# Linear attention and butterfly feed-forward on one core: a new slot table for the feed-forward work of the last four chunks

## What is computed

```python
qkv = x @ W_qkv                                  # 16 heads of 64
q, k = relu(q @ W_f + b_f), relu(k @ W_f + b_f)
kv  = einsum('bhnd,bhne->bhde', k, v)
out = einsum('bhnd,bhde->bhne', q, kv) / (einsum('bhnd,bhd->bhn', q, k.sum(2)) + 1e-6)
x   = layernorm(x + out.reshape(...) @ W_out + b_out)
h   = gelu(butterfly(x @ W_exp + b_exp, up_weights) + up_bias)      # 512 hidden
x   = layernorm(x + butterfly(h, down_weights) @ W_con + b_con + down_bias)
```

## The kernel before

| chunk | x1T_lo | up tiles | down | transpose_y, residual |
|---|---|---|---|---|
| 4 | 33 | 33, 34, 35, 36 | 37 | 38 |
| 5 | 37 | 37, 38, 39, 40 | 41 | 42 |
| 6 | 41 | 41, 41, 42, 42 | 43 | 44 |
| 7 | 45 | 45, 45, 45, 45 | 46 | 47 |

## Time and profile before

### The profile page before, as it was taken

One profiled execution on the slowest core, in us unless ns is written; L12 is line 12 of the kernel. 1 busy time (PEld: TensorE's weight loads), 2 busy tenths in 40 slices (PEclk: granted clock), 3 DMA queues, 4 the chain that ended last, 5 costly groups with the idle time before them and its releaser, 6 DMA issues.

```text
span 379.0 us, 5158 instructions
## 1 busy us (share of the span) xinstructions
PE 333.4 (88%) x1841; PEld 235.3 (62%) x1841; DVE 246.2 (65%) x489; ACT 173.0 (46%) x289; POOL 80.6 (21%) x77
## 2 busy tenths in 40 slices
PE   4898999299799999999999999999979788589481
PEld 3765677176567767777767675776856565356250
DVE  3536999999956384666518774685585783882613
ACT  2531344034455564674645464646546543434120
POOL 3080565896300002001001100110110110111201
PEclk9999999879989999999999999999999989659766
DMA  5940509333902800630450046006505607500000
GB/s 176 302 143 32 191 17 315 113 112 117 214 9 48 179 0 2 149 78 2 112 115 0 2 110 144 2 3 139 113 2 123 132 3 164 116 0 0 29 28 28
DMA packets 25089, 33.73 MB, mean 89 GB/s; under 512 B 3656, under 2 KB 13928, under 8 KB 25064
## 3 DMA queue, kind: packets, MB, share of 16 engines
q1 hardware_dynamic: 24904, 33.38, 34.6%
q10 hardware_dynamic: 160, 0.03, 0.0%
HBM read 31.04 MB, written 2.36 MB: 88 GB/s over the span
## 4 chain that ended last, share of the span: by engine, by line
PE 52%; DVE 28%; issue 7%; DMA 6%; POOL 4%; ACT 2%; SPq 1%; POOLq 0%; DVEq 0%
PE ring L483 18%; PE kx_ps L555 9%; PE attn_ps L483 8%; DVE late L914 6%; PE ring L643 5%; DMA recips<-recip_rows 4%; DVE qn L995 3%; POOL rstd L462 3%; DVE stats L1004 3%; PE ring L535 2%; PE ring L575 2%; DVE bias_row_term L930 2%; PE desk L492 2%; DVE k_total L969 2%; DVE y_dn L918 2%
## 5 line engine op out<-in xcount | busy, mean ns | idle before, releaser
L765 ACT ACTIVATE q<-ring,bf_col 128x512 f32<-128x512 f32 x64 | 43.9, 686 | 52.3 <-PE ring L483 51.9
L555 PE MATMUL kx_ps<-k,xs 128*128 128x512 f32 x128 | 60.2, 593 | 0.8 <-ACT k L758 0.8
L751 ACT ACTIVATE qn_h<-qn 128x512 fp32r<-128x512 f32 x64 | 39.8, 627 | 36.7 <-DVE qn L995 36.7
L758 ACT ACTIVATE k<-ring 128x512 f32<-128x512 f32 x64 | 38.3, 598 | 34.2 <-PE ring L535 33.8
L901 DVE TENSOR_TENSOR qn_l<-qn,qn_h 128x512 fp32r<-128x512 f32 x64 | 42.9, 680 | 15.8 <-ACT qn_h L751 15.0
L459 POOL TENSOR_TENSOR var_eps<-mean_var,ln_eps 128x4 f32<-128x4 f32 x16 | 7.1, 443 | 205.0 <-DVE mean_var L1008 205.0
L995 DVE TENSOR_TENSOR qn<-q,recips 128x512 f32<-128x512 f32 x64 | 41.1, 684 | 10.5 <-DMA recips<-recip_rows 10.5
L451 POOL TENSOR_TENSOR y<-hid,y_up 128x512 f32<-128x512 f32 x18 | 38.3, 2150 | 39.8 <-DMA hid<-in_L_ffn_up_weights_dram 39.7
L555 PEld LDWEIGHTS kx_ps<-k,xs 128*128 128x128 f32 x128 | 24.1, 189 | 19.2 <-issue 16.5
L483 PE MATMUL ring<-xT_h,wq_h 128*128 128x512 f32 x64 | 35.9, 561 | 0.0
L483 PE MATMUL attn_ps<-qn_h,m_h 128*128 128x512 f32 x64 | 29.2, 456 | 7.6 <-DVE qn_l L901 3.9
(11 more groups left out here) (125 smaller groups left out, 549.7 us busy)
## 6 DMA issues: line engine op xcount, KB each, us to landing
recips<-recip_rows SPq DMA_DIRECT2D x32, 512.0 KB, 7.3
hid<-in_L_ffn_up_weights_dram SPq DMA_DIRECT2D x9, 512.0 KB, 5.3
x<-_L_ffn_down_weights_dram SPq DMA_DIRECT2D x9, 512.0 KB, 4.1
xs<-in_L_attn_x_dram SPq DMA_DIRECT2D x4, 512.0 KB, 7.4
out_dram<-y SPq DMA_DIRECT2D x8, 256.0 KB, 6.1
q<-in_L_attn_W_qkv_dram SPq DMA_DIRECT2D x2, 512.0 KB, 7.9
q<-in_L_attn_W_qkv_dram SPq DMA_DIRECT2D x2, 256.0 KB, 3.3
q<-in_L_attn_W_out_dram SPq DMA_DIRECT2D x2, 256.0 KB, 8.8
```

The lines of the kernel that those rows point to most:

```text
L555: t_.matmul(kx_ps[half], xs[b % XBUF][:, t, :], k[kt % KRING][:, half * CH:(half + 1) * CH], start=t == 0, stop=t == TILES - 1).then_inc(s ...
L751: a_.activation(dst, src, ACT.Copy).then_inc(done, 1)
L758: a_.activation(k[kt % KRING][:, half * CH:(half + 1) * CH], bank(("k", kt, half))[:, :], ACT.Relu).then_inc(s_taken, 1)
L765: a_.activation(q[:, i % QRING, :], bank(("q", i))[:, :], ACT.Relu, bias=bf_col[:, :])\
```

## The change

The tables of chunks 0 to 3 stay as they were. Those of chunks 4 to 7 are given by hand:

```diff
-    for n in range(ALLCH):
-        per = [1, 1, 1, 1, 1, 1, 2, 4][n]
+    for n in range(ALLCH - 4):
         at = ATTN_LAST[n] + 3
         for i in range(HT):
-            UPS.setdefault(at + i // per, []).append(HT * n + i)
-        DOWN_SLOT[at + HT // per] = n
-        YT_SLOT[at + HT // per + 1] = n
+            UPS[at + i] = [HT * n + i]
+        DOWN_SLOT[at + HT] = n
+        YT_SLOT[at + HT + 1] = n
+
+    for n, ups, down, back in [(4, [33, 34, 35, 35], 36, 37), (5, [37, 37, 38, 38], 39, 43),
+                               (6, [41, 41, 42, 42], 43, 45), (7, [45, 45, 45, 45], 46, 47)]:
+        for i in range(HT):
+            UPS.setdefault(ups[i], []).append(HT * n + i)
+        DOWN_SLOT[down] = n
+        YT_SLOT[back] = n
```

## The result

367.87 us, median of 4 runs (366.48 to 369.69), against 381.08 (380.1 to 384.87, a fourth run of the kernel before added): ratio 0.9638, 95% interval 0.9559 to 0.9717. The two medians alone give 0.965. The forecast was 368.3 with a range of 364.8 to 374.8. The profiled execution took 367.46, its span is 365.6 (forecast 366.35, before 379.0). Lines after the tables have moved down by 6: L483 is L489 now, L643 is L649, L995 is L1001.

A forecast was written before the change was run, and what follows sets the result against it. VectorE and TensorE wait for each other by turns. The last up tiles start 10.35 us earlier and take 2.3 less: span 379.0 - 10.35 - 2.3 = 366.35, with 1.9 around it 368.3 us, range 364.8 to 374.8.

The forecast's parts named there:

- Slots 35 and 36: Extra up tile and down projection of chunk 4 come early: norm(7) ends at 310.5, x1T_lo at 317.35.
- Slot 37: Second norm of chunk 4, nearly free in the DMA wait; first qn at 322.9 instead of 321.38, 1.5 lost.
- Slot 38: Without a norm it takes 2.6 us on VectorE; the next slot begins at 325.5 instead of 328.17.
- Slot 39: VectorE's norm takes 6.8 us plus 0.2 waiting; down(5), from 327.2 to 330.7, is hidden and 4.69 us leaves the chain.
- Slots 40 to 42: Up tiles begin at 337.0; six products take 4.2 us plus 1.7 for half clock, to 342.9; before, 349.2.
- Slots 43 to 45: add_x(7) from 343.5, residual(5) behind it, x1T_lo to 350.6; last up tiles start at 351.1, 10.35 us earlier.
- The last up tiles: In slot 45, at full clock: 2.8 + 0.2 instead of 5.27 us, 2.3 less (bounds 0 and 2.5).
- down(5) isn't hidden: Rival: from slot 39 half clock until chunk 5's down projection is over, up tiles 5 later; 373.3 us, chance 0.13.
- Only the order at the end counts: Rival: TensorE's work bounds slots 38 to 42, only slots 43 to 45 are shortened; 376.9 us, chance 0.13.
- Half clock all through: Rival: the clock never comes back from slot 39 on; 386.4 us, 1.4% slower, chance 0.05.

The follow-up runs named there:

- e10: Changed kernel with 15 more matmuls, read by nobody, behind down(5) in slot 39; ratio to before 0.9715.
- e11: Changed kernel with chunk 5's up tiles in 37 to 40 and its down in 41, as before; ratio to before 0.9707.
- e1: Kernel before with chunk 4's part of the change alone (fourth up tile in 35, down in 36, back in 37); ratio to before 0.9897.
- e2: Kernel before with chunk 5's up tiles in 37 and 38 and its down in 39 alone; ratio to before 0.9918.
- e9: Changed kernel with chunk 4 as it was before (fourth up tile 36, down 37, back 38); ratio to before 0.9712.
- e13: Kernel before with 13, 4 and 2 more matmuls, read by nobody, at the ends of slots 38, 39 and 40; ratio to before 0.997.
- e6: Kernel before with 22 more matmuls, read by nobody, in TensorE's idle time of slot 44; ratio to before 0.9925.
- e12: Changed kernel with the ways back of chunks 5 and 6 in slots 42 and 44 as before; ratio to before 0.9855.
- e4: Changed kernel with chunk 6's way back in slot 44 again; ratio to before 0.9781.

## Why the prediction was right

The time, 367.87 against 368.3, and the mechanism hold. By its own steps, with what each measured:

- *Slots 35 and 36.* norm(7) from 308.92 to 310.9 (forecast end 310.5), x1T_lo of chunk 5 at 317.13 to 317.8 (317.35). Right, with everything 0.42 later from what lies ahead (309.41 for 308.99).
- *Slot 37.* The norm of chunk 4 outlasts the reciprocals, first qn at 323.37 (322.9). Right: a loss of 1.57 in distance (13.96 for 12.39), 1.5 forecast.
- *Slot 38* 2.59 (2.6). Right. Slot 39, which VectorE starts at 325.96 (325.5), lasts 7.33, not 7.0: qn_h kept it waiting 0.35 where I had 0.2, and the transposed attention 0.19, because the adds and transposes ran at half clock. Those also put down(5) off, which I had near 327 and which began at 329.40. That cost nothing more, since it was hidden, as e10 and e11 show.
- *Slots 40 to 42.* **This term was mis-sized.** I took 1.7 us for half clock from step 60 on; the clock was 1.00, and the six products took 4.21 us, so the term measured 0. transpose_attn(7) began at 342.13, not 342.9, although the up tiles had begun 0.9 late (337.92 for 337.0). The early down projection is not what brought the clock back. That happened in step 57, the last thing ahead of it (a matmul of 512 columns takes 0.63 at half clock and 0.39 at full):
```profile
328.68 0.63 PE L489 MATMUL attn_ps<-qn_l,m_h 128*128 128x512 f32 x1
329.11 0.46 PE L489 MATMUL attn_ps<-qn_h,m_l 128*128 128x512 f32 x1
```
  And e1 and e11, without an early down(5), also have 1.00 in slot 41, while e2 and e9, which have it but leave the layer norm of chunk 4 in slot 38, are near half there (0.56 and 0.50 from 336 to 340). So in these traces it goes with chunk 4's move, behind which TensorE waits less: its gaps from the head of slot 39 on VectorE to the up tiles of slot 41 come to 1.47 us here, 1.91 in e1 and 1.92 in e11, against 2.79 before, 2.87 in e2 and 3.07 in e9. I had treated the clock as a risk of the new order. The runs show that it is a part of the gain: before, half clock in slots 39 to 41 cost 2.5 us on the chain (e13).
- *Slots 43 to 45.* add_x at 342.77 (343.5), residual(5) right behind it, x1T_lo's end 7.04 later (7.1), at 349.8 for 350.6, transpose_y(6) 0.41 of TensorE ahead of the up tiles (0.5). Right.
- *The last up tiles* at full clock: down(7) begins 353.14 - 350.28 = 2.86 us after them (3.0). Right, and e6 shows that the 2.3 us were the clock's.

So 366.35 against a span of 365.6 is +0.42 from ahead of the change, +0.5 in slots 37 to 41, most of it in slot 39, -1.7 for the clock, and less than 0.1 behind. The errors in part cancelled. What the four moves are worth is not a sum: alone or undone alone they measure 5.5 or 4.4 (chunk 4; 3.1 without e9's late reciprocals), 3.3 or 1.9 (chunk 5 early), 7.3 (both ways back). My split by place was sound; a split by move depends on the order in which they are made. Part of the reason shows: chunk 4's move is worth 2.6 us by itself in both (2.62 in e1, 3.90 less 1.27 in e9), but it also brings the clock back, and that is worth 2.53 us behind slot 41's head while down(5) is on the chain (e1), and 1.1 when it isn't (e9).

The rivals: "down(5) isn't hidden" falls with e10 and e11. "Only the order at the end counts" falls with e1 and e2, which leave the end alone and are faster by about 1%, and it is partly true, since e12 puts 7.3 of 13.8 us there. "Half clock all through" falls with the stretches above. The fall that there is, at 324 to 328 (0.73), came with a wait of 2.32 us. The Trainium skill, "TensorE: Matmul & The Clock Gate", section "A second HAM failure mode: psum-queue depth-cycling", says that short idle times between groups of matmuls can be frequent enough to make the clock swing. The trace of the changed kernel does not agree for slots 40 to 45, where gaps of 0.69, 0.78, 0.78 and 1.41 us left the clock at 1.00. That of e9 does: its gaps of 0.81, 1.36 and 0.90 us went with a fall from 1.00 (328 to 332) to 0.50 (336 to 340).

## What to carry to other kernels

Where two engines wait for each other by turns, lay their timelines side by side and move independent work of the idle one to where the other is the bound, and short-chained work (a layer norm with a hop to a slow engine) either into a DMA wait or behind the last producer that the end needs. Price TensorE's work at the clock that its neighbours leave it: filling idle time can be worth more than the time that is filled, as it was in e1. With executions that vary by 1% ahead of the change, measure the distance from the last common instruction to the end as well.

## What was not expected of the hardware

In the order of before, 19 matmuls that nobody reads (13, 4 and 2 of them) in TensorE's idle time made the chain 2.5 us shorter behind them, and 22 made the last stretch 2.3 us shorter, without moving any instruction (both in the trace; the times don't settle it). And the clock in slots 35 and 36 was not the same in executions with the same order up to there: after a wait of 2.73 us for VectorE ahead of the head maps e11 had 0.74 in the stretch of 304 to 308 us, e10 after one of 2.72 had 1.00.

The store of the reciprocals, four small DMAs, is on the path to slot 38, and I had taken it as fixed. It was not: 1.44 us in the chain of e13, 3.14 in that of e4.
```profile
311.74 1.44 DMA recip_rows<-recip
```
```profile
311.01 3.14 DMA recip_rows<-recip
```
Most of the 1.27 us in e9 is this (2.61 there; in e2, with the same order up to slot 41, it is 1.44). The layer norm of chunk 4 in slot 37 hides part of such a delay.
